# Values through memory in fp32, and one row difference formed on another engine

## The reference

```python
x = x + _L0_conv_ref(_gn(x), L0_conv_w0, L0_conv_w1, L0_conv_w2, L0_conv_bias)
x = x + _L1_conv_ref(_gn(x), L1_conv_spatial_weight)
```

```python
sim = dot / jnp.maximum(norm_x[:, None] * norm_p, EPS)
likelihood = (sim + 1.0) * 0.5
weight = likelihood * spatial_weight[None, :, None, None]
out = jnp.einsum('bckhw,bkhw->bchw', patches, weight)
```

## Time and profile before

| | us |
|---|---|
| median of 3 runs | 2229.93 |
| lowest, highest | 2226.68, 2234.81 |
| the profiled execution | 2236.67 |
| its span | 2235.0 |
| VectorE busy | 1408.0 |
| TensorE busy | 1634.4 |
| granted TensorE clock, mean | 0.829 of full |

### The profile page before, as it was taken

How to read it: one execution, slowest core, us unless ns; L and a number is a source line. 1 busy time by engine, 2 the same in 40 slices (tenths; PEclk the granted TensorE clock), 3 DMA queues, 4 the chain that set the end, 5 groups by cost and what they waited for, 6 DMA issues and landing times.

```text
span 2235.0 us, 49426 instructions
## 1 busy us (share of the span) xinstructions
PE 1634.4 (73%) x16895; PEld 862.5 (39%) x16895; DVE 1408.0 (63%) x2121; ACT 738.2 (33%) x1222; POOL 448.3 (20%) x792
## 2 busy tenths in 40 slices
PE   5777777878578776888568785778678795875465
PEld 3543333434234343434234342335334352432243
DVE  6428646966378455966478554866479554875354
ACT  2321233423243233424233242423334242423341
POOL 1352422022301222012300232013300232011000
PEclk7888888989789897979788896989888896887566
DMA  5242446763857546673856556583766557572665
GB/s 164 75 125 75 122 129 152 185 171 92 192 141 192 140 126 167 157 186 99 189 149 183 134 133 167 140 207 99 172 162 174 139 131 178 139 197 76 146 164 135
DMA packets 151106, 329.95 MB, mean 148 GB/s; under 512 B 47092, under 2 KB 96244, under 8 KB 150260
## 3 DMA queue, kind: packets, MB, share of 16 engines
q1 hardware_dynamic: 109296, 207.18, 37.2%
q0 software_dynamic: 41472, 118.24, 20.1%
HBM read 238.70 MB, written 86.61 MB: 146 GB/s over the span
## 4 chain that ended last, share of the span: by engine, by line
PE 27%; DMA 21%; DVE 18%; SPq 17%; issue 11%; ACT 3%; DVEq 2%; POOL 0%; ACTq 0%; POOLq 0%
DMA d_n<-st_n 12%; PE conv L1300 8%; PE conv L1274 5%; DMA unit_mem<-d_n 5%; SPq L385 4%; DMA unit_mem<-d_hl 3%; SPq L413 3%; PE gram L1368 3%; PE conv L1259 3%; SPq L383 2%; PE out_ps L1393 2%; SPq L408 2%; SPq L405 2%; DVE wgt L1020 2%; PE stat_ps L1323 2%
## 5 line engine op out<-in xcount | busy, mean ns | idle before, releaser
L1020 DVE SCALAR_TENSOR_TENSOR wgt<-gram,tapw 124x512 f32<-124x512 f32 x512 | 350.4, 687 | 360.5 <-PE gram L1368 321.9
L1300 PE MATMUL conv<-thl,wconv 128*128 128x496 f16 (+2 forms) x1920 | 559.9, 422 | 16.8 <-DVE xa L899 9.6
L471 POOL DMA_DIRECT2D ring<-in_x x576 | 333.7, 584 | 475.3 <-DVE bn L781 244.1
L1368 PE MATMUL gram<-unit_mem 128*60 128x128 f16 x4096 | 264.8, 255 | 198.9 <-DMA unit_mem<-d_hl 122.8
L1368 PEld LDWEIGHTS gram<-unit_mem 128*60 128x60 f16 x4096 | 160.6, 118 | 428.9 <-issue 427.2
L1323 PE MATMUL stat_ps<-st_n,sq_c 128*128 128x306 f32 x256 | 123.0, 570 | 186.7 <-ACT st_n L556 153.7
L1300 PEld LDWEIGHTS conv<-thl,wconv 128*128 128x128 f16 x1920 | 171.2, 105 | 223.8 <-issue 81.3
L1274 PE MATMUL conv<-thl,wconv 128*128 128x480 f16 (+7 forms) x1200 | 255.3, 367 | 0.0
L1393 PE MATMUL out_ps<-wgt,vals 124*32 124x128 f32 x4096 | 195.2, 311 | 35.6 <-issue 31.5
L556 ACT ACTIVATE vals<-vals_ps 124x512 f32<-124x512 f32 x128 | 76.3, 596 | 391.5 <-PE vals_ps L1351 391.5
L505 POOL DMA_DIRECT2D up<-d_z x128 | 68.7, 539 | 560.4 <-DVE xa L951 500.5
(11 more groups left out here) (133 smaller groups left out, 2007.3 us busy)
## 6 DMA issues: line engine op xcount, KB each, us to landing
unit_mem<-d_hl SPq DMA_DIRECT2D x128, 360.0 KB, 6.5
unit_mem<-d_hl SPq DMA_DIRECT2D x256, 180.0 KB, 8.4
ring<-in_x POOLq DMA_DIRECT2D x288, 128.0 KB, 4.1
ring<-in_x POOLq DMA_DIRECT2D x288, 127.0 KB, 4.4
d_hl<-st_hl SPq DMA_DIRECT2D x128, 180.0 KB
d_v<-st_v SPq DMA_DIRECT2D x128, 180.0 KB
unit_mem<-d_v SPq DMA_DIRECT2D x64, 360.0 KB
up<-d_z POOLq DMA_DIRECT2D x160, 128.0 KB, 3.2
```

Of the source, the lines that this page charges most:

```text
L471: pool.dma_start(dst, src).then_inc(raw_in[slot], 16)
L1020: V.scalar_tensor_tensor(out=dst, in0=g, scalar=SIM_SCALE ** 2, in1=tapw[:, :].unsqueeze(1).to_broadcast([KN, 2, 2 * QN]), op0=ALU.add, op ...
L1300: last = mm(dst[:, :, b0:b1], wconv0[:, w, 2 * (p % ROWS4) + s, dx + 2, :], thl[:, p % 2, d, s, :, b0 + dx:b1 + dx] if p % ROWS4 != 1 else ...
L1368: last = mm(bank[row:row + KQ, col:col + QN], key[:, q, e_at, TH * KW * g:TH * KW * g + KQ], tile[:, :, TH * g + 1:TH * g + 1 + TH, 1:1 + ...
```

## The change

Values go through memory as fp32, in one piece: `st_v`, `d_v` and the values' part of `unit_mem` are fp32 (of the same size in bytes as the two fp16 halves). ScalarE's copy writes fp32; `value_lows` is gone, with its eight calls a batch; `unit_lows` waits for the copy instead. A save has four transfers, a load of values two (two quadrants go to 32 partitions each). TensorE's value products are fp32 on both sides, with as many instructions: the 64 partitions now hold quadrants 0, 1 and 2, 3, and `pick_c` has for each pair a 64 x 32 matrix which takes the right 32 rows.

`wino_delta(i, 1)` leaves VectorE. GpSimd does the copy and the subtraction in its stream between the second and the third `load_up`, as soon as `xa` is complete and point 3's input is formed; `wino_in` of point 4 waits for them.

```diff
-SAVES, LOADS, LATER = 80, 96, 80
+SAVES, LOADS, LATER = 64, 96, 96
-    unpair = np.zeros((2 * C, C), np.float16)
-    unpair[np.arange(2 * C), np.arange(2 * C) % C] = 1 / X_SCALE
+    pick = np.zeros((2 * C, 2, C), np.float32)
+    pick[np.arange(2 * C), np.arange(2 * C) // C, np.arange(2 * C) % C] = 1 / X_SCALE
-        st_v = sb("st_v", [P, 2, 2, FN], F16)
+        st_v = sb("st_v", [P, 2, FN], F32)
...
             # save_half
-                for hl in range(2):
-                    sp.dma_start(d_v[b, h, hl].rearrange("c q n -> q c n"), st_v[:, hl, h % 2, :]).then_inc(half_saved[h % 2], 16)
+                sp.dma_start(d_v[b, h].rearrange("c q n -> q c n"), st_v[:, h % 2, :]).then_inc(half_saved[h % 2], 16)
             # load_unit
-                sp.dma_start(values[s][0:2 * C].rearrange("c q e n -> c (q e n)"),
-                             d_v[b, u].rearrange("l c q n -> (l c) (q n)")).then_inc(rest_in[s], 16)
+                for t in range(2):
+                    sp.dma_start(values[s][C * t:C * t + C].rearrange("c q e n -> c (q e n)"),
+                                 d_v[b, u, :, 2 * t:2 * t + 2, :].rearrange("c q n -> c (q n)")).then_inc(rest_in[s], 16)
             # GpSimd's iteration
                     load_up(i, 1)
+                    pool.wait_ge(xn_done, CHUNKS * i + CHUNKS)
+                    pool.wait_ge(t_wide, 8 * i + 4)
+                    alone(pool)
+                    nc.gpsimd.tensor_copy(delta[:, 0:2, :], delta[:, DROWS - 2:DROWS, :]).then_inc(delta_step, 1)
+                    pool.wait_ge(delta_step, 2 * i + 1)
+                    alone(pool)
+                    nc.gpsimd.tensor_tensor(delta[:, 2:DROWS, :], xa[:, DROWS + 2:2 * DROWS, :],
+                                            xa[:, DROWS:2 * DROWS - 2, :], ALU.subtract).then_inc(delta_step, 1)
                     load_up(i, 2)
             # half_in
-                copy(in_strips(st_v[:, 0, half, :]), strips(part)).then_inc(v_high, 1)
+                copy(in_strips(st_v[:, half, :]), strips(part)).then_inc(v_kept, 1)
             # wino_in
                     dve.wait_ge(t_ready, 8 * i + p)
+                    if p == 4:
+                        dve.wait_ge(delta_step, 2 * i + 2)
             # unit_lows
                 dve.wait_ge(unit_high, 8 * b + h + 1)
-                dve.wait_ge(value_low, 8 * b + h + 1)
+                dve.wait_ge(v_kept, 8 * b + h + 1)
             # VectorE's iteration
-                            if k == 1 and j == 2:
-                                wino_delta(i, 1)
-                                if k == 0:
-                                    value_lows(b, h)
             # key_values
-                                      values[s][0:2 * C, q, e, TH * KW * g:TH * KW * g + KQ], unpair_c[:, :],
+                                      values[s][0:2 * C, q % 2, e, TH * KW * g:TH * KW * g + KQ], pick_c[:, q // 2, :],
```

More of the change, by code:

```diff
@@ L91 @@
 GN_LINKS = 5
-WINO_LINKS = 13
+WINO_LINKS = 11
 W0_TOTAL = W0_TILES * ROWS4
@@ L130, in host_constants @@
             taps[64 * (k % 2):64 * (k % 2) + KQ, t, k // 2] = (dr == t // K - K // 2) & (dc == t % K - K // 2)
-    return square, gather, taps.reshape(KN, TAPS * 2 * QN), unpair
+    return square, gather, taps.reshape(KN, TAPS * 2 * QN), pick
 def first(n):
@@ L153, in link, with build @@
         engine.wait_ge(self.sem, self.base + self.k)
-def build(nc, x, w0, w1, w2, bias, spatial, square, gather, tapmask, unpair, out):
+def build(nc, x, w0, w1, w2, bias, spatial, square, gather, tapmask, pick, out):
     ctx = ExitStack()
@@ L196, in build @@
         gat_c = sb("gat_c", [P, Q, P], F32)
-        unpair_c = sb("unpair_c", [2 * C, C], F16)
+        pick_c = sb("pick_c", [2 * C, 2, C], F32)
         bn1, bn2 = sb("bn1", [P, CONV_TILES, 6], F32), sb("bn2", [P, CONV_TILES, 6], F32)
@@ L218, in unit_part @@
             return unit_mem[:, s, n * Q * FN:(n + 1) * Q * FN].rearrange("p (q e n) -> p q e n", q=Q, e=GROUPS)
-        keys, queries, values = ([unit_part(s, n) for s in range(2)] for n in range(3))
+        keys, queries = ([unit_part(s, n) for s in range(2)] for n in range(2))
+        values = [unit_mem[:, s, 2 * Q * FN:3 * Q * FN].bitcast(F32).rearrange("p (q e n) -> p q e n", q=2, e=GROUPS) for s in range(2)]
         norm_strips = [unit_mem[:, s, 2 * Q * FN:3 * Q * FN].bitcast(F32).rearrange("p (e n) -> p e n", e=2) for s in range(2)]
@@ L244, in build @@
         d_hl = dram("d_hl", [B, 2 * BANDS, 2, C, Q, FN], F16)
-        d_v = dram("d_v", [B, 2 * BANDS, 2, C, Q, FN], F16)
+        d_v = dram("d_v", [B, 2 * BANDS, C, Q, FN], F32)
         d_n = dram("d_n", [B, 2 * BANDS, Q, UN], F32)
@@ L277, in build @@
         wino_link = sem("wino_link")
+        delta_step = sem("delta_step")
         t_wide, t_high, t_ready = sem("t_wide"), sem("t_high"), sem("t_ready")
@@ L298, in build @@
         sq_done = sem("sq_done")
-        v_high = sem("v_high")
+        v_kept = sem("v_kept")
         n2_ready = sem("n2_ready")
@@ L306, in build @@
         unit_high = sem("unit_high")
-        value_low = sem("value_low")
         unit_low = sem("unit_low")
@@ L372, in _ @@
             sp.dma_start(spat[:, :], spatial.rearrange("(a k) -> a k", a=1).to_broadcast([P, TAPS])).then_inc(const_in, 16)
-            sp.dma_start(unpair_c[:, :], unpair).then_inc(const_in, 16)
+            sp.dma_start(pick_c[:, :, :], pick).then_inc(const_in, 16)
             sp.wait_ge(wmixed, 7)
@@ L850, in wino_delta @@
                     wino_chain.link(dve, V.tensor_tensor(delta[:, :, :], xa[:, 2:DROWS + 2, :], xa[:, 0:DROWS, :], ALU.subtract))
[L851 to L855, removed]
             def wino_in(i, p, step=None):
@@ L978, in units_close @@
                                        op0=ALU.mult, op1=ALU.mult).then_inc(unit_vec, 1)
-            def value_lows(b, h):
-                dve.wait_ge(v_high, 8 * b + h + 1)
-                V.tensor_tensor(in_strips(st_v[:, 1, h % 2, :]), strips(image_of(h)), in_strips(st_v[:, 0, h % 2, :]),
-                                ALU.subtract).then_inc(value_low, 1)
             def unit_lows(b, h):
                 dve.wait_ge(unit_high, 8 * b + h + 1)
-                dve.wait_ge(value_low, 8 * b + h + 1)
+                dve.wait_ge(v_kept, 8 * b + h + 1)
                 V.tensor_tensor(in_strips(st_hl[:, 1, h % 2, :]), strips(st_b[:, :]), in_strips(st_hl[:, 0, h % 2, :]), ALU.subtract).then_inc(unit_low, 1)
@@ L1542, in const_arrays @@
 def const_arrays():
-    return dict(zip(("square", "gather", "taps", "unpair"), host_constants()))
+    return dict(zip(("square", "gather", "taps", "pick"), host_constants()))
 _INS = ["x", "L0_conv_w0", "L0_conv_w1", "L0_conv_w2", "L0_conv_bias", "L1_conv_spatial_weight"]
```

## The result

| | before | after |
|---|---|---|
| median (us) | 2231.93 (4 runs) | 2315.71 (4 runs) |
| lowest, highest | 2226.68, 2234.81 | 2298.20, 2326.97 |
| the profiled execution | 2236.67 | 2298.2 |

The change makes the kernel slower: the ratio is 1.0371, 95% interval [1.0302, 1.044]. 84 us were added where 5 less were forecast.

A forecast was written before the change was run, and what follows sets the result against it. No engine was taken as full: batches were split by stage among VectorE, TensorE and landings. Terms -20 (VectorE relief) + 16 + 4 (fp32 products) - 6 (saves) = -6, rounded to -5: 2225 us from 2229.9; range 2207 to 2244.

The forecast's parts named there:

- The size of a burst: TensorE's bursts of 32 value products: fp32 doubles 0.58 us, 0.58 more; bounds about 0.35 and 1.16 more.
- 16 fp32 products of the output take 0.57, 36 ns each: TensorE's fp32 output burst, taken as a neighbour to size the fp32 value products at double the old 18 ns.
- rival B: Slower: a value burst costs three times the old one; +14, 2244 us; decides from 0.94 us more a burst; chance 0.18.
- against B: The evidence given against the tripled value burst: the fp32 output burst, 16 products in 0.57 us.
- the last batch's 4: Last batch, without convolution, at the half clock: four value bursts in the open, 4 us lost.
- The cover of units 0 to 5: Value bursts in units 0 to 5 stand beside idle TensorE, priced at nothing; without cover 7 us more an iteration.
- in the open: Four value bursts of units 6 and 7, where only TensorE sets the pace: 2.3 us an iteration, 16 lost.
- The row differences: Copy and subtraction moved from VectorE to GpSimd: unit 2 gains 2.0 us an iteration.
- The hold: VectorE's wino_low in unit 2 waits until GpSimd finishes: gain 2.2 us if GpSimd takes 3.7, 0.3 if 5.6.
- The value lows and the saves: Value lows off VectorE: 0.85 us an iteration, in unit 4; DMA saves: 0.25 us each, 6 us in all.
- Units 0 and 1 shorter by more than 1 us: Sign of a wrong forecast: a wait there was VectorE's own; removing the value lows there was priced at 0.
- d_n landing 7.6 us after its issue: Sign of a right forecast: before the units, a save's last transfer lands 7.6 us after issue; 7.88 before.

The follow-up runs named there:

- e3: Kernel after, but value products read keys and a constant in fp16, so values don't reach the output: 2194.6 us, ratio 0.9817 to before.
- e4: Kernel after with half as many fp32 value products, each of 64 columns for two quadrants with the same weights: 2223.48 us, ratio 0.9961 to before.
- e13: Kernel of e3 with each burst of fp16 value products done twice: 2264.93 us, ratio 1.0159 to before.
- e7: Kernel of e3 with fp32 value products in units 0 to 5 only: 2253.23 us, ratio 1.0095 to before.
- e6: Kernel of e3 with fp32 value products in units 6 and 7 only: 2244.83 us, ratio 1.0045 to before.
- e2: Kernel before with only the row differences' copy and subtraction moved to GpSimd: 2232.81 us, ratio 1.0012 to before.
- e5: Kernel of e4 with the row differences back on VectorE: 2223.31 us, ratio 0.9953 to before.
- e12: Kernel of e3 with the row differences back on VectorE: 2199.96 us, ratio 0.9861 to before.
- e1: Kernel after with the row differences back on VectorE, the values' part alone: 2294.53 us, ratio 1.0284 to before.
- e9: Kernel of e4 with GpSimd's subtraction in four pieces of 512 columns: 2217.07 us, ratio 0.9939 to before.

## Why the prediction was wrong, by its steps

The 121 us of the fp32 products divide along the runs: e3 to e4, longer pairs in the same number, +29; e4 to e13, the same burst from twice the pairs, +41; e13 to the kernel after, the same number of longer pairs, +51. This is a path through kernels, and another path could divide the 121 otherwise: in the kernel after TensorE's stops are 15 us more than in e4, in e13 56 more.

- **The size of a burst: the step that failed first.** "16 fp32 products of the output take 0.57, 36 ns each": the 16 of the earlier trace rows are records of the trace. `filter_group` issues 8 matmuls (2 values of c, 4 bands). `norm_piece` is one fp32 matmul, and the earlier trace rows shows it as x2. At 72 ns for each of the code's products, 32 of them are 2.3 us, beyond the forecast's upper bound of 1.74 and past rival B's point of decision; 1.88 was measured, +1.30 for the forecast's +0.58. What stood "against B", the fp32 output burst, was for it, once its count is read against the code. The forecast's own sum with +1.30 is -20 + 36 + 9 - 6 = +19, an estimate in which the last batch's 4 grows as the 16 does. So this step alone turns the sign, and doesn't make the 84.
- **The number of instructions: a term that the forecast did not have.** It took the change to have as many instructions. It has 8252 more. e13 and e4 put 41 us on that where the pairs are short; how much of it is in the kernel after, whose pairs are long, is not shown.
- **The cover of units 0 to 5.** Those bursts were priced at nothing as long as TensorE idles beside them; e7 has 59 us. At +1.30 twelve bursts in eight batches are 125 us of products, so half of it was covered. By stage the cover held in units 0 and 1 (0.5 us an iteration) and failed in units 2 to 5 (6.8), which the prediction had described by unit 5 with TensorE busy 14.96 of 21.70. Unit 5 is 23.1 there, 22.8 after and in e13, and 18.7 and 19.2 in e3 and e4. The number of instructions can't be all of that either, since unit 5 took 21.5 before, with the fewest instructions. The four bursts of units 6 and 7 cost 50 in e6; 4 x 8 x 1.30 is 42: that they are in the open was right.
- **The row differences: 20 us shed, nothing gained.** GpSimd's time was bounded rightly (2.3 to 5.6, measured 4.5). The hold was placed rightly and sized too small: 3.1 us in unit 2. GpSimd began when it was to begin, 0.65 us behind the points of unit 3. But wino_low came 1.9 us behind them and not 3.5 as before, because the value low (0.86) and a wait for a gram (0.83) no longer stood in front of it, and so more of GpSimd's 4.5 us was still to come. From wino_low's start to the next weights it was 4.19 us before (1409.85 to 1414.04) and 4.28 after (1421.82 to 1426.10): 2.0 forecast, nothing gained. The runs say 0 (e2 against before, e4 against e5, e3 against e12). By the Trainium skill's 4497 ns (GPSIMD Engine Reference, section 3.1) and its lock (SBUF — State Buffer, "SBUF: two separate sides") the working gave 1.4 an iteration; it took wino_low where it stood before, and the trace doesn't agree with the 1.4.
- **The value lows and the saves: too small.** Together they were to give 12 us; e12 has 32. "Units 0 and 1 shorter by more than 1 us" was to show a fault of the sum: together they are 2.5 us shorter after, 2.8 in e3 and 3.2 in e12, and units 2 to 5 another 2.8 in e3, where 0.85 for the value lows was forecast. The way is the one that the prediction named and sized at 0.25 a save: `half_in` waits for the save of two heights before. Averaged over six iterations, the third save of a batch lands 67.1 us after the first one was issued, 70.6 before: 3.5 an iteration, against 0.75. The prediction had sized it from the save of height 0, which runs with little beside it, and that one gains nothing: 11.9 us from its first issue to its landing, 11.2 before. Those of heights 1 and 2 run beside loads, and they fall from 20.3 to 17.9 and from 19.7 to 15.8. In that of height 1 SyncE's queue needed 7.27 us for its two issues of `d_v`, and needs 0.90 for the one (before, then after):

```profile
1333.20 7.27 SPq L385 DMA_DIRECT2D d_v<-st_v  x2
...
1349.46 0.90 SPq L387 DMA_DIRECT2D d_v<-st_v  x1
```

How much of the 32 us is the save's and how much the value lows', no run separates. A packet of 1440 bytes takes 61 to 65 ns in the median, one of 2880 takes 114. The sign named for it, d_n landing 7.6 us after its issue, missed: before the units it lands 9.3 us or more after, and it is issued only 0.7 us sooner. (The 86 GB/s read there is the mean of all queues in that window; the queue of the earlier trace rows moved 0.75 MB in the 12 us.)
- **The sum, re-made with measured terms.** -32 for the values' way and +121 for the products, 0 for GpSimd: +89, against 84 measured. With e4's burst in it, -32 and +29, it is -3, and e4 is at -6.

Right was GpSimd's duration. VectorE's busy time was to fall by 77 and fell by 48.7: 18 came back as wino_low's holds and 4 as that of `tapw`, and the rest is overlap of neighbouring records, which the page counts once.

Open: how more and longer pairs come to lengthen unit 5 by 4 us, in which TensorE idles; why the border of units 0 and 1 moves by 5; e1's 21 us below the whole change; and the 8 us of e6 above its products' time. These are measured, not their way. The parts of e6 and e7 add up to 109 of the 121.

## What to carry to other kernels

Hold every count of a profile row against the count in the code before dividing by it: a count twice the code's is what the operation costs in instructions. Where a change multiplies the instructions of an engine, price the number apart from the time; the old work done twice (e13) measures it for short instructions. When a stage gets shorter, look at the next one before counting a gain: 5 us of unit 0 were in unit 1 again. Before work goes to GpSimd, look at what VectorE does in the microseconds after: GpSimd held it here with a subtraction that reads two tiles, memsets did not, and smaller pieces held it less (0.8 for 1.9 us in the mean). Taking work away in front of that VectorE operation can bring it under the hold.

## What the runs showed of the hardware

- An fp32 matmul is two pairs of weight load and product in the program (8192 records for 4096 in the code, 57678 for 49426 instructions), with 64 and 128 rows and with 32 and 60 columns of weights.
- Such a pair with 64 moving columns takes what it takes with 32: 27.1 ns with 60 columns of fp32 weights. It takes 15.6 with 32 columns of weights, and an fp16 pair with 60 takes 14.5. So e4, which does two quadrants on one load, halves the pairs at the same 27.1 ns each: +0.46 us a burst for +1.30.
- TensorE stops for 1 to 4.4 us (mean 2.2 in e13) with nothing to wait for, mostly ending about 1.5 us after a packet of 16384 bytes of instructions: 22 times in e4, 36 before, 35 after, 55 in e13.
- The hold works in both directions: where VectorE's value low began 0.08 us before it, e2's GpSimd subtraction took 5.2 us, and 4.5 in iteration 0 and in the kernel after. In e9 the piece that wino_low preceded took 2.24 us, and 1.26 the others.
